# Adjacency loads of 1 MB in place of 512 KB in a two-layer graph kernel: one load and one semaphore for each two of four slots

## The reference

```python
def _L0_gnn_ref(h, adj, W):
    Wh = h @ W.T
    norms = jnp.linalg.norm(Wh, axis=1, keepdims=True)
    sim = Wh @ Wh.T / (norms * norms.T + EPS)
    mask = (adj > 0) | jnp.eye(N, dtype=bool)
    alpha = jax.nn.softmax(jnp.where(mask, sim, -jnp.inf), axis=1)
    return alpha @ Wh
def _L1_gnn_ref(x, adj, W_self, b_self, W_nb, b_nb, W_comb, b_comb):
    mask = (adj > 0).astype(x.dtype)
    agg = mask @ x / jnp.maximum(jnp.sum(mask, axis=1, keepdims=True), 1.0)
    combined = jnp.concatenate([x @ W_self + b_self, agg @ W_nb + b_nb], axis=-1)
    return jax.nn.relu(combined @ W_comb + b_comb)
x = _layernorm(x + _L0_gnn_ref(x, adj, L0_gnn_W), axis=-1)
x = _layernorm(x + _L1_gnn_ref(x, adj, ...), axis=-1)
```

## Time and profile before

| | before |
|---|---|
| median of 3 runs | 845.5 us (844.79 to 845.76) |
| profiled execution: device time | 845.18 us |
| profiled execution: span of the core | 843.3 us |
| PE busy | 822.8 us (98%) |
| DVE busy | 589.7 us (70%) |
| ACT busy | 343.4 us (41%) |
| adjacency loads | 128 of 512 KB, median 4.9 us from issue to landing |
| part-0 and part-1 transposes | 112, median 3.7 us to landing |

### The profile page before, as it was taken

The page is one execution under the profiler, slowest core; times in us unless marked ns, Lnnn a source line. Parts: engine busy times, 40 slices in busy tenths (PEclk is TensorE's granted clock), DMA queues, the critical chain, the costliest instruction groups (busy, mean ns, idle before and its releaser), DMA issues.

```text
span 843.3 us, 17681 instructions
## 1 busy us (share of the span) xinstructions
PE 822.8 (98%) x6591; PEld 655.8 (78%) x6591; DVE 589.7 (70%) x1472; ACT 343.4 (41%) x553; POOL 73.8 (9%) x177
## 2 busy tenths in 40 slices
PE   8999999799999999999999999999999999999997
PEld 6866777577777777777777777778888888888886
DVE  2888978788787888888798989998254333333333
ACT  4866656365555655555556555554100000000000
POOL 2400000000000000001000102021111100110011
PEclk9999999999999999999999999999999999999999
DMA  8969999869999799979998989996103330330300
GB/s 217 246 156 233 272 230 233 183 216 232 254 224 241 222 259 246 233 228 245 257 272 204 239 249 235 240 245 219 26 13 132 118 110 23 120 118 15 120 19 20
DMA packets 223469, 155.26 MB, mean 184 GB/s; under 512 B 159905, under 2 KB 186802, under 8 KB 222354
## 3 DMA queue, kind: packets, MB, share of 16 engines
q1 hardware_dynamic: 223186, 153.68, 70.4%
q0 software_dynamic: 192, 0.41, 0.3%
HBM read 95.83 MB, written 20.99 MB: 139 GB/s over the span
## 4 chain that ended last, share of the span: by engine, by line
issue 76%; POOL 6%; DVE 1%; POOLq 1%; ACT 0%; DVEq 0%; ACTq 0%
POOL rstd L585 4%; POOL var_eps L583 2%; POOLq L584 0%; POOLq L582 0%; DVE mgroup L1039 0%; ACT mgroup L700 0%; DVE work L1015 0%; POOLq L587 0%; ACT work L644 0%; DVE prob_lo L1021 0%; DVE mix_extremes L860 0%; ACT mask L684 0%; ACT feat L730 0%; DVE prob_hi L1020 0%; POOL mix_extremes_dram L576 0%
## 5 line engine op out<-in xcount | busy, mean ns | idle before, releaser
L1281 PE MATMUL ps<-feat,prob_hi 128*128 128x257 f16 x1024 | 281.3, 275 | 9.8 <-DVE prob_lo L1021 6.6
L1283 PE MATMUL ps<-feat,prob_lo 128*128 128x257 f16 x1024 | 280.2, 274 | 0.0
L1282 PE MATMUL ps<-feat,prob_hi 128*128 128x256 f16 x1024 | 279.1, 273 | 0.0
L1410 PE MATMUL ps<-big,mgroup 128*128 128x257 f16 x992 | 219.2, 273 | 0.0
L1411 PE MATMUL ps<-big,mgroup 128*128 128x256 f16 x992 | 219.2, 273 | 0.0
L684 ACT ACTIVATE mask<-work 128x1024 fp8e4<-128x1024 f16 x112 | 114.9, 1048 | 100.3 <-DVE work L1015 100.3
L1281 PEld LDWEIGHTS ps<-feat,prob_hi 128*128 128x128 f16 x1024 | 99.9, 98 | 39.0 <-DVE prob_lo L1021 9.0
L644 ACT ACTIVATE work<-ps 128x512 f32<-128x512 f32 (+2 forms) x144 | 80.0, 557 | 100.4 <-PE ps L1234 99.5
L1282 PEld LDWEIGHTS ps<-feat,prob_hi 128*128 128x128 f16 x1024 | 100.8, 98 | 25.0
L1039 DVE SCALAR_TENSOR_TENSOR mgroup<-work,mgroup 128x512 f16<-128x512 f32 x112 | 77.1, 689 | 52.3 <-ACT mgroup L700 51.3
L1283 PEld LDWEIGHTS ps<-feat,prob_lo 128*128 128x128 f16 x1024 | 99.6, 97 | 14.0
(11 more groups left out here) (126 smaller groups left out, 795.1 us busy)
## 6 DMA issues: line engine op xcount, KB each, us to landing
adj_sb<-adjT SPq DMA_DIRECT2D x128, 512.0 KB, 4.9
mask_spill<-mask SPq DMA_DIRECT2D x128, 128.0 KB, 4.7
mgroup<-mask_spill SPq DMA_DIRECT2D x8, 2048.0 KB, 8.0
xres<-x SPq DMA_DIRECT2D x8, 512.0 KB, 5.1
out<-rows SPq DMA_DIRECT2D x32, 128.0 KB, 1.7
feat<-xT SPq DMA_DIRECT2D x7, 512.0 KB, 7.2
mgroup<-mgroup SPq DMA_TRANSPOSE x112, 3.7
norm_bc<-norm_row_dram SPq DMA_DIRECT2D x7, 256.0 KB, 6.2
```

Of the source, the lines that this page charges most:

```text
L1281: pe.matmul(acc(D + 1), prob_hi[:, s, cols], feat_hi_of(g)[:, r, 0:D + 1], start=start, stop=False)
L1282: pe.matmul(acc(D), prob_hi[:, s, cols], feat_lo_of(g)[:, r, :], start=False, stop=False)
L1283: return pe.matmul(acc(D + 1), prob_lo[:, s, cols], feat_hi_of(g)[:, r, 0:D + 1], start=False, stop=stop)
L1410: pe.matmul(agg_ps(q, D + 1), lhsT, z_hi_of(g)[:, r, 0:D + 1], start=(jb == 0), stop=False)
```

## The change

`adj_loaded` has two semaphores, one for slots 0 and 1 and one for slots 2 and 3. A load brings both units of such a half, 1 MB, in one DMA. On SP it is issued under m odd alone, after the keep of the half's second unit, in a diagonal after its fourth tile is masked. DVE waits for the semaphore of the half before either unit. The loads of the start are merged in the same way.

```diff
-        adj_loaded = [sem(f"adj_loaded{i}") for i in range(4)]
+        adj_loaded = [sem(f"adj_loaded{i}") for i in range(2)]
...
-            def load_direct(a, b, m, slot):
-                sync.dma_start(adj_sb[:, slot, :].rearrange("p (s i) -> p s i", s=2),
-                               adjT_v[b, :, 2 * m:2 * m + 2, a * GW:(a + 1) * GW]).then_inc(adj_loaded[slot], 16)
-
-
-            def load_next(a, b, m, slot):
-                if m < 2:
-                    load_direct(a, b, m, slot)
-                else:
-                    load_direct(b, a, m - 2, slot)
+            def load_blocks(a, b, u):
+                half = u // 2 % 2
+                sync.dma_start(adj_sb[:, 2 * half:2 * half + 2, :].rearrange("p t (s i) -> p (t s) i", s=2),
+                               adjT_v[b, :, :, a * GW:(a + 1) * GW]).then_inc(adj_loaded[half], 16)
...
-                    load_direct(0, 0, 0, 0)
-                    load_direct(0, 0, 1, 1)
-            load_direct(0, 1, 0, 2)
-            load_direct(0, 1, 1, 3)
+                    load_blocks(0, 0, 0)
+            load_blocks(0, 1, 2)
...
-                    if a + 1 < G:
-                        sync.wait_ge(prob_ready, t0 + 2 * m + 2)
-                        load_next(a, a + 1, m + 2, slot)
+                    if m == 1 and a + 1 < G:
+                        sync.wait_ge(prob_ready, t0 + GB)
+                        load_blocks(a + 1, a, u0 + 4)
                     sync.wait_ge(mask_ready, u0 + m + 1)
...
                     if m < 2:
                         turn_far(a, b, m)
-                    sync.wait_ge(kept_ready, 4 * k + m + 1)
-                    if b < G - 1:
-                        load_next(a, b + 1, m, slot)
-                    elif m < 2:
-                        load_direct(a + 1, a + 1, m, slot)
-                    elif a + 2 < G:
-                        load_next(a + 1, a + 2, m - 2, slot)
+                    if m % 2:
+                        sync.wait_ge(kept_ready, 4 * k + m + 1)
+                        if b < G - 1:
+                            load_blocks(*((a, b + 1) if m == 1 else (b + 1, a)), u0 + m + 3)
+                        elif m == 1:
+                            load_blocks(a + 1, a + 1, u0 + 4)
+                        elif a + 2 < G:
+                            load_blocks(a + 1, a + 2, u0 + 6)
                     sync.wait_ge(mask_ready, u0 + m + 1)
...
-                dve.wait_ge(adj_loaded[u_slot], loaded)
+                dve.wait_ge(adj_loaded[u_slot // 2], loaded)
...
-                dve.wait_ge(adj_loaded[u % 4], 16 * (u // 4 + 1))
+                dve.wait_ge(adj_loaded[u // 2 % 2], 16 * (u // 4 + 1))
```

## The result

| | before | after |
|---|---|---|
| median | 845.63 us (844.79 to 845.78) | 905.28 us (904.41 to 906.83) |
| ratio | | 1.071, 95% interval 1.069 to 1.073 |
| span of the profiled execution | 843.3 us | 902.6 us |
| PE busy | 822.8 us, 98% | 834.4 us, 92% |
| adjacency loads | 128 of 512 KB, median 4.9 us | 64 of 1 MB, median 6.2 us |

59.7 us slower; the forecast was 52 us.

What follows compares the result with a forecast made beforehand. TensorE was taken as the bound, with unit 0's load the one without room. First late loads 17 us, later pairs 23, row 0's five 12: 52 us on 845.5, say 898 us, range 872 to 938.

Steps and rivals of the forecast that it cites:

- The bound and the one load without room: TensorE busy 822.8 of 843.3 us; the next pair's unit 0 load lands only 0.3 us before DVE's keep.
- The price of a 1 MB load: Adjacency load on SP: 4.3 us plus 1.6 for the second 512 KB, 5.9 us; bounds 5.1 and 7.7.
- the forecast's own factor of 21: Merged loads of units 0 and 1: each 1 us of landing time costs 21 us in all.
- The loop: Keep 0 to next pair's keep 0: DVE 9.5, transposes 2.7, load 5.9; 18.1 us against 15.75, 2.3 more a pair.
- 18.8 against 16.4: Row 0's keep-to-keep loop, 18.8 us instead of 16.4: 2.4 us for each of 5 pairs, 12 us.
- the 0.7 us of room: Load a row's last pair issues for the next diagonal: lands at 364.7, first use 365.38; seven such places, no cost.
- The clock rival: PE's clock halves after idling, 1.7 us at each of six row ends, 10 us; with slower loads 908 to 938, chance 0.18.
- PE's busy time: Sign of being right: TensorE's busy time stays at 823 us while its share falls to 92%.
- The lead of PE: At tile x = 2 the part is ready 2.0 us before PE starts it; taken off the first stall, 4.8 to 2.8.
- Not slower: Rival: unit 0's stall stays within PE's 2.0 us, needing a load landing within 3 us of issue; 845.5 us, chance 0.03.
- faster by batching: Rival: 64 fewer issues on SP stop delaying the transposes, at most 6.6 us of PE's waits; 839 us, chance 0.02.
- Only the first load of a row: Rival: DVE's stretch shrinks to about 7 us, so later loads lose nothing; 17 us, 862; with halves, chance 0.10.

Runs made afterwards that it cites:

- experiment 1: Changed kernel's load places, but two loads of 512 KB with four semaphores instead of one of 1 MB: 867.97 us, 1.026 against the kernel before.
- 3: Kernel before with 1 MB loads for the diagonals and for units 2 and 3 alone: 845.62 us, 1.0003 against the kernel before.
- 4: Kernel before with 1 MB loads for units 0 and 1 alone: 903.85 us, 1.068 against the kernel before.
- experiment 9: Changed kernel, unit 1's keep right behind unit 0's, merged load of units 0 and 1 ahead of both pairs of transposes: 843.89 us, 0.996 against the kernel before.
- experiment 2: Kernel before, 512 KB loads at their old places, but one semaphore per half, so DVE waits for both units: 882.74 us, 1.043.
- experiment 8: Changed kernel, both keeps early, load between the pairs of transposes, mixing-weight extremes one pair earlier: 860.28 us, 1.013 against the kernel before.
- 5: Changed kernel with the 1 MB load of units 0 and 1 issued ahead of the part-1 transposes: 863.23 us, 1.021 against the kernel before.
- 6: Changed kernel with unit 1's keep right behind unit 0's and the load issued between the two pairs of transposes: 856.92 us, 1.013 against the kernel before.

## Why the prediction was right, point by point

**The bound and the one load without room** were read rightly: 21 waits of 4.64 us on average (97.5 / 21), "4 to 5 us each, some 90 us in all". Experiments 1, 3 and 4 bear it out: merging costs only where the load has no room; there the place alone costs 22 us and the size 37 more.

**The price of a 1 MB load** was 5.9 us in the forecast from two neighbouring landings, and 5.9 in the turn above; the 21 that a keep 0 waits for took 6.08 on average, which by the forecast's own factor of 21 is 3.8 us of the 7.7 us that it fell short. The median of all 64 is 6.2. The Trainium skill's 6.15 us for 1 MB (page DMA: Bandwidth & Descriptors, section Bandwidth), given there for loads that GpSimd issues and without the time of the issue, is near this. Its rule to issue early and wait late (section Rules for kernel authors) is what experiment 9 restores: `keep` waits 0.2 us there, against 97.8.

**The loop** was forecast at 18.1 us and is 18.1 in (2,6). The sum by rows, from the delay of PE's first attention matmul in each diagonal against the kernel before (worked out from PE's timelines: 16.5, 32.3, 42.3, 49.8, 56.0 and 59.3 us for a = 1 to 6, with -0.4 at a = 0):

| row a | forecast, us | measured, us |
|---|---|---|
| 0 | 2.8 + 12 = 14.8 | 16.9 |
| 1 | 2.8 + 4 x 2.3 = 12.0 | 15.9 |
| 2 | 9.7 | 9.9 |
| 3 | 7.4 | 7.5 |
| 4 | 5.1 | 6.2 |
| 5 | 2.8 | 3.3 |

Of the 7.7 us missing, 6.0 are in rows 0 and 1. *Row 0*: the term "18.8 against 16.4" took one pair's 16.4 us; PE's own pace there was 80.9 us for five pairs, 16.2, and the loop was 19.0. *Row 1*: PE's delay, read at its first matmul on tile x = 2 of each pair, grows by 1.8 us in the first stall (forecast 2.8) and by 12.0 in the four loops (forecast 9.2). The last two loops took 19.3 and 18.8 us. SP's timeline shows the issue of these two loads taking longer, and they landed after 6.9 us:

```profile
265.16 1.49 SPq L389 DMA_DIRECT2D adj_sb<-adjT  x1
...
283.99 1.65 SPq L389 DMA_DIRECT2D adj_sb<-adjT  x1
```

Why these two is open, but it isn't the change's doing alone: at the same two places the 512 KB load behind the transposes took 5.5 and 4.9 us to land in the kernel before and 5.0 and 5.1 in experiment 1, where its neighbours in the row took 4.3 to 4.6. The row's last pair loads for diagonal 2; that load landed after 7.1 us, the diagonal's first tile started 0.08 us behind it, and PE's delay grew by 0.4 us. So the 0.7 us of room that the forecast had there was used up, as it was, by 0.1 us each, ahead of diagonals 4 and 5. The remaining 1.7 us of row 1 are the clock's, next.

**The clock rival** had a small part. Windows of the changed kernel at the three places that had no half clock before (clock is the third number from the end):

```profile
71.50:76.00 4.50, 3.87 (x17) 2.37 (x18) 4.50 (x11) 1.11 (x2) 0.00 (x0) 0.62 0.32 118
...
256.00:260.00 4.00, 4.00 (x18) 2.02 (x16) 3.96 (x11) 0.60 (x1) 0.00 (x0) 0.57 0.27 51
293.50:297.50 4.00, 4.00 (x18) 2.23 (x17) 4.00 (x11) 0.73 (x2) 0.00 (x0) 0.57 0.25 58
```

PE was granted 1.2 GHz for 3.4 us in each: from 72.0 on, as a wait of 2.44 us ended (at 72.13), from 256.3 on, 1.1 us behind one of 2.20 (to 255.21), and from 293.9 on, 0.5 us behind one of 2.86 (to 293.33). I had held such waits against this rival as half too short; these three were not, and they are three of the four longest behind a late load. Each costs 1.7 us of PE's work. Behind the first two comes another stall, whose end the load sets and not PE, so it swallows them. Behind the third, the last of its row, there is none, and PE's rows show the loss: from the first matmul on tile x = 2 to the first on x = 3, without a wait between, 2.62 us before and 4.30 after.

```profile
263.07 0.27 PE L1281 MATMUL ps<-feat,prob_hi 128*128 128x257 f16 x1
...
265.69 0.27 PE L1281 MATMUL ps<-feat,prob_hi 128*128 128x257 f16 x1
```

```profile
293.33 0.28 PE L1274 MATMUL ps<-feat,prob_hi 128*128 128x257 f16 x1 [2.86 <-DVE prob_lo L1014]
...
297.63 0.27 PE L1274 MATMUL ps<-feat,prob_hi 128*128 128x257 f16 x1
```

(the upper fence is the kernel before, the lower the changed one). This is the forecast's mechanism, a loss only at the end of a row, once instead of six times. The upper end of this rival was added up wrongly: 936 + 10 is 946, not 938.

**PE's busy time** was to stay at 823 us and is 834.4; the share of 92% came out all the same. The three half-clock stretches are 5 us of the 11.6. The rest is, by an estimate, a matter of how records are counted: a matmul's record lasts 0.27 us while the next starts 0.11 us later, so each new break in PE's work leaves 0.16 us more on record, and there are 43 more breaks, 7 us.

**The lead of PE**, 2.0 us, was spent as forecast: PE waits 1.97 us at x = 2 where DVE waits 4.48, and the last 0.3 us of the loop's surplus of 2.3 go to the copies behind it. "PE's wait for `prob_lo` near 55 us" came out as 48.1, with 5.3 more for the copies (`big`, L997) that stand in the same queue.

**Not slower** and **faster by batching** are out by the result, and experiment 9 shows what the first would have needed: the load's place, not its size. The forecast's remark that "its place in the loop excludes" it holds of the change as made only. **Only the first load of a row** would have given 17 us. The first late loads cost 1.8 to 2.9 us each by the start of pair (a, a + 2) (PE's delay, worked out likewise), and 3.3 by the end of row 5, which has no other; the later ones cost the rest, some 40 us.

**Where the working was weak** is SP's own time: I gave the two transposes a fixed 2.7 us. In the changed kernel that held (2.6 us, at most 2.9), since no load stood close in front of them. Where one does, their issue takes up to 4.1 us behind 512 KB (experiment 2) and up to 7.5 behind 1 MB (experiment 8), and this term missed in 2, 5 and 6.

## What to carry to other kernels

For a load, ask for each user of its bytes when the last byte is wanted, and from which instruction of the issuing queue it now leaves: merging two loads moves the earlier one to the place of the later, behind all that is queued between. Where the loads are in a loop with the work that frees their slots, write the loop out (work, issue, landing) and compare it with the bound engine's time for a turn; the difference is paid in each turn, the first stall less the lead once. A merged load is free if it goes out in a gap of the issuing queue and its slots are free by then: here that took a keep of unit 1 moved forward on DVE and a place ahead of both transposes.

## What the runs showed of the hardware

The issue of a pair of part-1 transposes on SP, over the 28 pairs of each trace, by what SP had issued before it:

| kernel | last adjacency load before | issue, us: median (range) |
|---|---|---|
| changed | 1 MB, 10 us or more earlier, landed | 2.6 (2.6 to 2.9) |
| before | 512 KB, mostly 1 to 3 us earlier | 2.9 (2.6 to 4.0) |
| experiment 2 | 512 KB, mostly 1.9 us earlier | 2.8 (2.6 to 4.1) |
| experiment 5 | 1 MB, mostly 1 to 2 us earlier | 4.3 (2.6 to 6.4) |
| experiment 8 | 1 MB, mostly 1.3 to 2.6 us earlier | 4.9 (3.3 to 7.5) |

With a load on its way a DMA transpose on this queue is held up already at its issue, and not in its data alone; by how much varies from pair to pair, and what decides it is open. Nor had I expected waits of PE of 2.20, 2.44 and 2.86 us to be followed by 3.4 us at 1.2 GHz; one of 2.24 us (ending at 236.79) was not, and none of the many of 1.97 us or less.
